# Layer 1 of a two-layer graph kernel reassociated, (A h) W in place of A (h W), with 512-wide matmuls

## What is computed

```python
h = jnp.maximum(_layernorm(x, axis=-1), 0.0)
Xw = h @ Wv + bv
sj = Xw @ aw[:d, 0]
si = Xw @ aw[d:, 0]
e = jax.nn.leaky_relu(sj[:, None, :] + si[:, :, None] + ab[0], negative_slope=0.2)
alpha_matrix = A * jnp.exp(e)
transition = alpha_matrix / (jnp.sum(alpha_matrix, axis=-1, keepdims=True) + 1e-12)
# H = sum over k of (transition^k h) @ Wk[k] + bk[k], for k = 0, 1, 2
x = x + jax.nn.relu(H)
h = jnp.maximum(_layernorm(x, axis=-1), 0.0)
Ah = A + jnp.eye(N)
dh = jax.lax.rsqrt(jnp.sum(Ah, axis=-1))
An = dh[:, :, None] * Ah * dh[:, None, :]
x = x + jax.nn.relu(jnp.einsum('bnm,bmf,fc->bnc', An, h, kernel) + bias)
```

## Time and profile before

| | us |
|---|---|
| median of 3 runs | 867.5 (867.31 to 870.92) |
| the profiled execution's own time | 868.26 |
| its span, first to last instruction | 866.5 |
| PE busy | 795.5 (92%) |
| DVE busy | 649.6 (75%) |
| ACT busy | 509.9 (59%) |
| POOL busy | 367.3 (42%) |
| DMA moved | 128.70 MB, mean 149 GB/s |

### The profile page before, as it was taken

How to read it: one execution, slowest core, us unless ns; L and a number is a source line. 1 busy time by engine, 2 the same in 40 slices (tenths; PEclk the granted TensorE clock), 3 DMA queues, 4 the chain that set the end, 5 groups by cost and what they waited for, 6 DMA issues and landing times.

```text
span 866.5 us, 15910 instructions
## 1 busy us (share of the span) xinstructions
PE 795.5 (92%) x6092; PEld 762.3 (88%) x6092; DVE 649.6 (75%) x1375; ACT 509.9 (59%) x997; POOL 367.3 (42%) x279
## 2 busy tenths in 40 slices
PE   2957999899989999899998999989998999999998
PEld 2757898898989999898998989889898999989998
DVE  4558597966979669885879759797697966986565
ACT  2488555676467654674647745567646765468232
POOL 1025154462355432652437515446235543275416
PEclk9968999999999999999999999999999999999999
DMA  5436341871428533574317834187143751256502
GB/s 182 146 120 196 134 129 44 254 246 61 135 84 252 201 98 98 153 257 157 114 52 223 272 102 128 44 255 244 62 134 88 250 210 37 99 164 205 187 30 98
DMA packets 65227, 128.70 MB, mean 149 GB/s; under 512 B 6272, under 2 KB 32256, under 8 KB 65152
## 3 DMA queue, kind: packets, MB, share of 16 engines
q1 hardware_dynamic: 55936, 94.13, 33.1%
q10 hardware_dynamic: 9216, 33.56, 13.0%
HBM read 119.28 MB, written 8.39 MB: 147 GB/s over the span
## 4 chain that ended last, share of the span: by engine, by line
PE 55%; DVE 27%; DMA 6%; issue 5%; ACT 5%; POOL 2%; ACTq 0%; DVEq 0%
PE da L818 12%; PE acc L907 12%; PE acc L909 11%; PE acc L908 11%; DVE tg_e L615 5%; PE db L818 5%; DVE a_raw L658 4%; DVE p L644 4%; DVE h L567 3%; DMA x_res<-x_dram 3%; DMA out_dram<-o_tile 2%; PE tp L810 2%; DVE p L639 2%; DVE ht_lo L586 2%; ACT t_hi L401 2%
## 5 line engine op out<-in xcount | busy, mean ns | idle before, releaser
L907 PE MATMUL acc<-g_hi,t_hi 128*128 128x256 f32 (+1 forms) x1024 | 294.6, 288 | 17.4 <-issue 10.6
L909 PE MATMUL acc<-g_hi,t_lo 128*128 128x256 f32 (+1 forms) x1024 | 291.4, 285 | 0.0
L908 PE MATMUL acc<-g_lo,t_hi 128*128 128x256 f32 x1024 | 290.2, 283 | 0.0
L309 POOL TENSOR_TENSOR a_lo<-a_raw,a_hi 128x512 fp32r<-128x512 f32 x128 | 186.3, 1473 | 176.9 <-ACT a_hi L442 175.4
L907 PEld LDWEIGHTS acc<-g_hi,t_hi 128*128 128x128 f32 x1024 | 195.6, 191 | 17.7 <-issue 10.7
L908 PEld LDWEIGHTS acc<-g_lo,t_hi 128*128 128x128 f32 x1024 | 195.8, 191 | 0.0
L909 PEld LDWEIGHTS acc<-g_hi,t_lo 128*128 128x128 f32 x1024 | 195.7, 191 | 0.0
L907 PE MATMUL acc<-g_hi,a_hi 128*128 128x256 f32 x512 | 149.2, 291 | 21.7 <-POOL a_lo L309 21.6
L909 PE MATMUL acc<-g_hi,a_lo 128*128 128x256 f32 x512 | 146.2, 285 | 0.0
L908 PE MATMUL acc<-g_lo,a_hi 128*128 128x256 f32 x512 | 146.1, 285 | 0.0
L391 ACT ACTIVATE tg_e<-si,sij 128x256 f32<-128x256 f32 x256 | 110.0, 500 | 56.4 <-POOL t_lo L315 52.7
(11 more groups left out here) (87 smaller groups left out, 1545.4 us busy)
## 6 DMA issues: line engine op xcount, KB each, us to landing
tg_a<-adj_t_dram ACTq DMA_DIRECT2D x64, 512.0 KB, 4.0
a_raw<-adj_dram SPq DMA_DIRECT2D x64, 512.0 KB, 4.6
a_raw<-adj_t_dram SPq DMA_DIRECT2D x64, 512.0 KB, 5.1
h<-x_dram SPq DMA_DIRECT2D x8, 1024.0 KB, 5.4
x_res<-x_dram SPq DMA_DIRECT2D x64, 128.0 KB, 3.7
out_dram<-o_tile SPq DMA_DIRECT2D x64, 128.0 KB, 3.4
p<-wk_dram SPq DMA_DIRECT2D x1, 768.0 KB, 7.2
p<-bk_dram SPq DMA_DIRECT2D x1, 384.0 KB, 7.5
```

Source lines behind the costliest of these rows:

```text
L309: nc.gpsimd.tensor_tensor(a_half(a_lo, i, h), a_raw[:, i % RS, h * N // 2:(h + 1) * N // 2], a_half(a_hi, i, h).bitcast(F32), ALU.subtract ...
L907: nc.tensor.matmul(acc[:, s, 0:n], l_hi, r_hi, start=(jt == 0), stop=False)
L908: nc.tensor.matmul(acc[:, s, 0:D], l_hi, r_lo, start=False, stop=False)
L909: ins = nc.tensor.matmul(acc[:, s, 0:n], l_lo, r_hi, start=False, stop=(jt == NT - 1))
```

## The change

Layer 1 is computed as (A h) W. After V, ACT makes h and its scaled high part from x (`h1_part`: two dependent activations), DVE the low part (`hs_low`). The transposes and `layer1_dense` before Z are gone. In Z the stationary operand is a 128x128 block of scaled h, the moving operand 512 columns of transposed adjacency: 16 pieces q of six matmuls (`layer1_piece`), pieces 0 to 7 for the first 512 rows into both banks of `da`, 8 to 15 for the others into both of `tp`. The result is z transposed; `zt_round` and `zt_low` split it, and W is multiplied last, in eight `out_chunk`s of six matmuls of 256 columns into the single bank `db`: chunks 0 to 3 after pieces 10 to 13, chunks 4 to 7 after chunks 1 to 4 of the next batch's U. T is stored in units of half the rows: the leaky relu is two instructions of 512 columns in place of four of 256, chunk 0 of U waits for four units and chunk 4 for all eight. The queues of SP, ACT, DVE and POOL are laid out anew. h of layer 0 (`h0`) and scaled h of layer 1 share one buffer, and `tmp` takes the place of `g1_tmp` and `h1`. The host lays the transposed adjacency out as `adj_z`, whose chunk is one run of 4 KB per partition, of the same bytes in all.

```diff
...
     T_D = {2: HALVES[0:1], 3: HALVES[1:2]}
-    T_V = {-1: HALVES[2:3], 1: HALVES[3:4], 2: HALVES[4:5], 3: HALVES[5:6], 4: HALVES[6:7]}
-    T_Z = {i: HALVES[7 + i:8 + i] for i in range(8)}
-    T_U = {i: HALVES[15 + i:16 + i] for i in range(3)}
-    BEFORE_U = 15
...
-    ROWS_U = {0: (0,), 1: (1,), 2: (2,), 3: (3, 4), 4: (5, 6), 5: (7,)}
...
-    DIAG_Z = {0: 4, 1: 5, 3: 6, 4: 7}
...
-    A_FIRST = {i: (i + 2, 1) for i in (0, 2, 3, 4, 5)} | {1: (4, 0)}
-    A_THEN = {0: (3, 1)} | {i: (i + 3, 0) for i in (2, 3, 4)}
+    T_V = {1: HALVES[2:3], 4: HALVES[3:4], 5: HALVES[4:5], 6: HALVES[5:6], 7: HALVES[6:7]}
+    T_Z = dict(zip((1, 3, 5, 6, 8, 10, 11, 13, 15), (HALVES[7 + i:8 + i] for i in range(9))))
+    T_U = {0: HALVES[16:17], 1: HALVES[17:18]}
+    BEFORE_U = 16
...
+    ROWS_U = {2: (0, 1), 3: (2,), 4: (3, 4), 5: (5, 6), 6: (7,)}
+    STATS_U = {2: (0, 1, 2, 3), 3: (4, 5, 6, 7)}
...
+    OUT_Z = {10 + i: i for i in range(PB)}
+    OUT_U = {1 + i: PB + i for i in range(PB)}
...
+    DIAG = (0, 1, NT - 2, NT - 1)
...
+        zt = [da, tp.rearrange("p g k i -> p g (k i)")]
+        zt_hi = ht_hi.rearrange("p g k i -> p g (k i)")
+        zt_lo = ht_lo.rearrange("p g k i -> p g (k i)")
...
+            def load_row(b, t):
+                if t >= RS:
+                    sp.wait_ge(rows_done, b * NT + t - RS + 1)
+                elif b > 0:
+                    sp.wait_ge(a_ready[1], (b - 1) * NT + NT - RS + t + 1)
+                sp.dma_start(a_raw[:, t % RS, :], adj_v[b, :, t]).then_inc(raw_loaded[t % RS], 16)
...
+                    sp.wait_ge(a_ready[1], b * NT + i - RS + 1)
+                sp.dma_start(a_raw[:, i % RS, :], adj_z[b, i]).then_inc(raw_loaded[i % RS], 16)
...
+                if b > 1:
+                    sp.wait_ge(a_used[1], (b - 1) * NT)
...
+            for b in range(B):
+                for i in range(RS):
+                    if b > 0:
+                        store(b - 1, PB + i)
+                    load_row(b, RS + i)
                 for i in range(RS):
                     load_chunk(b, i)
-                if left > 1:
+                for i in range(NT):
+                    load_x_res(b, i)
+                    if i in (RS, RS + 1):
+                        load_chunk(b, i)
+                load_chunk(b, RS + 2)
+                load_chunk(b, RS + 3)
+                for i in range(PB):
+                    if b + 1 < B:
+                        load_row(b + 1, i)
+                    store(b, i)
+                if b + 2 < B:
                     load_h0(b + 2)
...
+                act.wait_ge(raw_loaded[i % RS], 16 * (b * (2 * NT // RS) + NT // RS + i // RS + 1))
+                if i in DIAG:
+                    act.wait_ge(diag_done, b * len(DIAG) + DIAG.index(i) + 1)
+                if b * NT + i >= 2:
+                    act.wait_ge(a_used[h], b * NT + i - 1)
+                nc.scalar.copy(piece(a_hi, i % 2, h), piece(a_raw, i % RS, h)).then_inc(a_hi_done[h], 1)
+            def h1_part(b, m):
+                if m % 2 == 0:
+                    act.wait_ge(nb1_ready, b * NG + m // 2 + 1)
...
+                    act.wait_ge(hs_ready, b * NT + m - 1)
+                nc.scalar.activation(tmp[:, m % 2, :], p0[:, b % 2, m, :], ACT.Relu, bias=nb1[:, m:m + 1],
+                                     scale=rstd1[:, m:m + 1]).then_inc(h1_ready, 1)
+                if m == 0:
+                    act.wait_ge(dh_ready, b + 1)
+                act.wait_ge(h1_ready, b * NT + m + 1)
+                nc.scalar.activation(hs_hi[:, m, :], tmp[:, m % 2, :], ACT.Copy,
+                                     scale=dh[:, m:m + 1]).then_inc(hs_hi_done, 1)
+            def zt_round(b, r):
+                act.wait_ge(a_used[1], b * NT + (r + 1) * PB)
+                for d in range(KD):
+                    nc.scalar.copy(zt_hi[:, d, :], zt[r][:, d, :]).then_inc(zt_hi_done, 1)
...
+                for i in range(NT):
+                    if i == 0 and b > 0:
+                        zt_round(b - 1, 1)
+                    t_steps(b, T_U.get(i, ()))
+                    if i == NT - 1 and more:
+                        transposed_hi(b + 1, 0)
+                    act.wait_ge(g1_tmp_ready, b * NT + i + 1)
+                    nc.scalar.copy(g1_hi[:, i, :], tmp[:, i % 2, :]).then_inc(g1_hi_done, 1)
+                    for t in ROWS_U.get(i, ()):
+                        rows(b, t)
...
+                for i in range(NT):
+                    if i == 0:
+                        if more:
+                            si_copy(b + 1, NG - 1)
+                        a_round(b, 1, 0)
+                        a_round(b, 1, 1)
+                    if more:
+                        t_steps(b + 1, T_V.get(i, ()))
+                    if i >= 3:
+                        h1_part(b, i - 3)
+                for q in range(NP):
+                    if q < 3:
+                        h1_part(b, NT - 3 + q)
+                    if q == NP // 2:
+                        zt_round(b, 0)
+                    if q + 3 in range(4, NP):
+                        a_round(b, (q + 3) // 2, (q + 3) % 2)
+                    if more:
+                        t_steps(b + 1, T_Z.get(q, ()))
+            zt_round(B - 1, 1)
...
+            def hs_low(b, m):
+                dve.wait_ge(hs_hi_done, b * NT + m + 1)
+                nc.vector.scalar_tensor_tensor(out=hs_lo[:, m, :], in0=tmp[:, m % 2, :], scalar=dh[:, m:m + 1],
+                                               in1=hs_hi[:, m, :].bitcast(F32), op0=ALU.mult,
+                                               op1=ALU.subtract).then_inc(hs_ready, 1)
...
+            def zt_low(b, r):
+                for d in range(KD):
+                    dve.wait_ge(zt_hi_done, (2 * b + r) * KD + d + 1)
+                    nc.vector.tensor_tensor(zt_lo[:, d, :], zt[r][:, d, :], zt_hi[:, d, :].bitcast(F32),
+                                            ALU.subtract).then_inc(zt_ready, 1)
+            def out_chunk(b, i):
                 s = i % 2
-                dve.wait_ge(acc_full, b * PHASES + 2 * NT + i + 1)
-                nc.vector.scalar_tensor_tensor(out=z_tmp[:, s, :], in0=acc[:, acc_slot(Z_PHASE, i), 0:D], scalar=dh[:, i:i + 1],
+                dve.wait_ge(out_full, b * NT + i + 1)
+                if b * NT + i >= 2:
+                    dve.wait_ge(stored[s], 16 * (b * (NT // 2) + i // 2))
+                nc.vector.scalar_tensor_tensor(out=o_tile[:, s, :], in0=db[:, 0:D], scalar=dh[:, i:i + 1],
                                                in1=bias1[:, :], op0=ALU.mult, op1=ALU.add).then_inc(z_tmp_done, 1)
...
+                for i in range(NT):
+                    if i == 0 and b > 0:
+                        zt_low(b - 1, 1)
+                    if i == NT - 1 and more:
+                        transposed_lo(b + 1, 0)
+                    u_chunk(b, i)
+                    if b > 0 and i - 1 in OUT_U:
+                        out_chunk(b - 1, OUT_U[i - 1])
...
+                        if i == NORM_U:
+                            dve.wait_ge(rstd0_ready, b + 2)
+                            norm0(0)
+                            norm0(1)
...
+                for i in range(NT):
+                    v_chunk(b, i)
+                    if i % 2:
+                        moments(b * NG + i // 2 + 1, st1, mv1, ve1, stats1, mean1, ve1_ready, (i - 1, i))
+                    elif i > 0:
+                        bias_of_norm1(b, i // 2 - 1)
+                    if i >= 3:
+                        hs_low(b, i - 3)
+                    if more:
+                        t_steps(b + 1, T_V.get(i, ()))
+                bias_of_norm1(b, NG - 1)
+                for q in range(NP):
+                    if q < 3:
+                        hs_low(b, NT - 3 + q)
+                    if q in (3, 4):
+                        diag(b, q + 3)
+                    if q == NP // 2:
+                        zt_low(b, 0)
+                    if q - 1 in OUT_Z:
+                        out_chunk(b, OUT_Z[q - 1])
+                    if more:
+                        t_steps(b + 1, T_Z.get(q, ()))
+            zt_low(B - 1, 1)
+            for i in range(PB):
+                out_chunk(B - 1, PB + i)
...
             def layer0_dense(b):
+                if b > 0:
+                    pe.wait_ge(g1_tmp_ready, b * NT)
...
+            def out_chunk(b, i):
+                pe.wait_ge(zt_ready, (2 * b + i // PB + 1) * KD)
+                if i > 0:
+                    pe.wait_ge(z_tmp_done, b * NT + i)
+                c = slice(i % PB * P, (i % PB + 1) * P)
+                split_product(db, D, [(zt_hi[:, d, c], zt_lo[:, d, c], wl_hi[:, d, :], wl_lo[:, d, :])
+                                      for d in range(KD)]).then_inc(out_full, 1)
+            def layer1_piece(b, q):
+                r, jt, c, h = q // NT, q % NT, q // 2, q % 2
+                pe.wait_ge(a_ready[h], b * NT + c + 1)
+                if r == 0:
+                    pe.wait_ge(hs_ready, b * NT + jt + 1)
```

(20 more changed lines are left out.)

707 lines of the change are left out of this document (237 added, 470 removed).

## The result

The changed kernel takes **959.0 us** (median of 4 runs, 957.1 to 964.4) against 868.0 (867.3 to 870.9) for the kernel before, measured alternately on the same chip: a ratio of 1.1055, 95% interval 1.101 to 1.110. It is slower, by 91 us. The forecast was 969, the range 870 to 1010.

A forecast was written before the change was run, and what follows sets the result against it. PE was taken to set the pace in 66 of 103 us a batch, and a chain over ACT, DVE and POOL in Z. The terms summed to +101.5 us on the profiled 868.3, giving 969 us, range 870 to 1010.

The forecast's parts named there:

- Beginning: Start of the kernel: wider leaky relu steps shorten ACT's chain for T that PE waits for; -3 us (0 to -5).
- W in U: Four W chunks become extra PE work in each of seven U stages, 2.9 us each time; +20 us.
- Waits for `db`: In U, PE waits three times a batch until DVE has read the single bank; 4.5 us a batch, +31.5.
- the walk of Z: Z followed through the engines' queues, every tie given to POOL; it ended at 42.7 us, and 39 was taken.
- From U to D0: D0's head waits for `u_chunk(7)`, whose row load stands behind a store; 4 us a batch, +25 in all.
- Z: Layer 1 stage, taken as 39 us against 37.1: +2 a batch (-5 to +6), +14 in all.
- Clock: Lower granted clock behind the new waits, two losses of 0.8 us a batch: +1.6 a batch, +11 in all.
- End: Last batch: layer 1 shorter, -5 us; then a tail of z's split and four W chunks, 9.6 us, +8.
- the minimum of 32.1 us: Z's lower bound: piece 9, behind chunk 6's load, at 19.3 us without lag, then 12.8 of PE work.
- first rival: Only the shortest chains hold: DVE keeps pace in V, Z takes 32.1 us, no clock loss; 890 us, chance 0.25.
- second rival: PE's work decides, chunk 6's load doesn't hold piece 9, Z about 26 us; 848 us, chance 0.17.
- The port: DVE and POOL hinder each other; DVE's lag at V's end grows, and `hs_low` with two SBUF inputs worsens it.

The follow-up runs named there:

- e1: The changed kernel with the W chunks alternating between the two banks of `da` in place of the single bank `db`: 912.0 us.
- e2: The changed kernel with SP issuing each row tile's load before the store of the W chunk, in place of after it: 943.6 us.
- e3: The changed kernel with the identity added to chunks 6 and 7 at q = 7 and 8 in place of 3 and 4: 960.3 us.
- e14: e10 with Z's W chunks one piece later and three half steps of T moved from Z to U: 879.1 us.
- e11: The changed kernel with POOL subtracting only 128 of each 512 columns of the adjacency's low part, the other terms left out: 946.3 us.
- e8: The changed kernel with two banks, row loads first, last bias first, a later `g1_tmp` wait, and pieces prepared at q + 4 in place of q + 3: 880.4 us.
- e10: e8 with the identity added to chunks 6 and 7 at q = 6 and 7 in place of 3 and 4: 885.4 us.
- e15: e14 with the identity of chunks 6 and 7 added back at q = 3 and 4: 892.0 us.

## Why the prediction was right, step by step

The sign and the size were right, and the profile shows every wait that was named: in U before `out_chunk` three times a batch, at D0's head, before pieces 4, 5 and 9. That the sum came within 10 us is in part luck: two of its terms are wrong by over 20 us each, in opposite directions. Measured between the two profiled executions, whose spans differ by 89.7:

- **Beginning**, forecast -3: 0. D0 of batch 1 starts at 88.72 before and at 88.78 after. PE waits 17.0 us for `t_lo` ahead of its first chunk of U, since that chunk now needs four whole units. T's last low part is ready at 75.0, before it was 81.3, so the shorter leaky relu did its work. I had not priced the new condition on chunk 0, which lets PE start its first chunk only at 58.6, in place of 53.1, and which stands in the change.
- **W in U**, +20: as forecast. A chunk takes 0.71 to 0.72.
- **Waits for `db`**, +31.5: 7 x 3 x 1.45 = 30.5 in U. e1 confirms the cause. Ten more of them, 10.3 us, lie in Z (seven) and at the end (three); there the walk of Z and the tail had them.
- **From U to D0**, +25: 18.1, seven waits of up to 3.2. The kind is right (e2). From batch 1 on the wait is 2.6 to 3.2 us where I took 4; the rows land after 4.1 us where I took 4.6, and the rest of the difference isn't traced.
- **Z**, forecast +2 a batch, from a walk to 42.7: +0.5, and 3.4 us of the 37.6 are the clock. Without clock losses Z is 34.2, so the walk was 8 us too long and the value taken, 39, 5 too long. The bias of the last norm came at V's end + 6.2, not 7.9 (DVE starts it at 368.21), piece 5 at 12.7 (14.1), piece 9 at 21.9 (24.4). I had let every tie go against Z.
- **Clock**, +1.6 a batch: 1.5 in D0 and 3.4 in Z of batch 2, three times as much. Over the seven batches it is 29 us in Z and 7.5 in D0, against 11. I had misread. The stretch 256 to 262 with its 0.87 doesn't lie behind the stall of 2.1 us; the stall is in it and ends at 260.35. Cut there, the kernel before shows the lower clock behind this stall too, for 3.2 us, a loss of 1.6 and not of 0.8:

```profile
260.35:262.00 1.65, 1.65 (x8) 1.65 (x9) 1.65 (x3) 0.46 (x2) 1.27 (x1) 0.51 1.07 383
262.00:263.30 1.30, 1.30 (x8) 1.30 (x8) 1.30 (x2) 1.30 (x4) 0.80 (x1) 0.50 0.91 212
```

So this term is some 26 us too small and the one under Z some 35 too large (7 x 5), and most of the two cancels.
- **End**, -5 + 8 = +3: from V's end to the end of the span 956.2 - 915.6 = 40.6 against 866.5 - 831.7 = 34.8, +5.8. Layer 1 of the last batch is 27.0 against 31.5, as forecast; from the last matmul of Z to DVE's last instruction it is 11.5 in place of the 9.6 that I had, again by the clock:

```profile
949.18 0.55 PE L699 MATMUL db<-wl_hi,ht_hi 128*128 128x256 f32 x1 [0.67 <-DVE o_tile L591]
951.47 0.55 PE L699 MATMUL db<-wl_hi,ht_hi 128*128 128x256 f32 x1 [0.67 <-DVE o_tile L591]
```

The last W chunks start 2.29 apart, of which only 0.67 is wait; their matmuls start 0.21 apart where it is 0.12 at full clock.

By stages the difference of 89.7 us is: beginning and batch 0 -0.1; U of batches 1 to 7 with the waits behind it 241.3 against 7 x 23.8, +75; six D0, 119.7 against 6 x 19.1, +5; V +0.3; six Z, 225.2 against 6 x 37.1, +3; end +6. Of U's 75, 20 is work, 30.5 the bank and 17 the wait for D0, by the list of waits. Of the other 7 us, 5 are the 0.24 by which each of the 21 waits for the bank costs more than the list says (see e1), and 1 is the same at D0's head (0.17 each). One is left.

**The steps that failed** are the reading of the clock, above, and the one under Z that said that chunk 6's load, `diag`, product and rounding make the minimum of 32.1 us. The chain is there, link by link, and it does set piece 9. But it isn't what alone sets the length of Z: taken away (e3), Z stays. The first rival (890 us) priced Z at 32.1, a length that only e14 comes near (32.7), in which three T steps are gone from Z, the waits for `db` are gone and the lead is longer. The second rival let the whole kernel decide at this one point ("where piece 9 comes before 13 us"). Piece 9 comes at 21.9, so its condition wasn't met. In e3, where piece 9 doesn't wait, it still comes 20.9 us behind V's end, as piece 5 waits longer, and the kernel is as slow: to free chunk 6's chain is not enough.

**The port**: "lag grows rather than shrinks" was wrong as a forecast. The lock itself is there after too: a step of DVE with two SBUF inputs took 2.09 us beside POOL's instruction of 2.39, like the earlier trace rows, and 0.43 alone. This agrees with the Trainium skill (SBUF — State Buffer, section Who interferes with whom), which says that a VectorE instruction with two SBUF inputs contends with a GpSimd instruction that reads SBUF, and that whichever of the two issues first decides who blocks. (POOL's had begun first, at 353.67, DVE's at 354.26.) But the new layout has fewer collisions. DVE's product took 1.67 us on average before and takes 1.30, the addition of the identity 1.04 and now 0.36, and `hs_low`, the new instruction with two SBUF inputs that I had held against the edit, takes 0.51 against the 0.48 of `l1_low` (its shortest is 0.48). Three groups of DVE in the changed kernel, with shapes, count, busy time and mean ns:

```profile
L522 DVE TENSOR_TENSOR tg_e<-tg_a,tg_e 128x1024 f32<-128x1024 f32 x64 | 82.9, 1296 | 6.3 <-ACT tg_e L354 6.2
...
L566 DVE SCALAR_TENSOR_TENSOR hs_lo<-tmp,dh,hs_hi 128x256 fp32r<-128x256 f32 x64 | 32.9, 514 | 26.4 <-ACT hs_hi L398 26.4
L577 DVE TENSOR_TENSOR a_raw<-a_raw,ident 128x128 f32<-128x128 f32 x64 | 20.2, 356 | 46.8 <-DMA a_raw<-adj_z_dram 46.8
```

The last row's 46.8 us of DMA wait is what e3 took away, at no gain.

**What is shown and what is argued.** Shown: the bank (e1, 47 us), the row load (e2, 15.5 us), that with the early identity POOL's split isn't what holds Z (e11), and that the late identity pays only with fewer steps of T in Z (e3, e8, e10, e14, e15). Argued: that the reason is two chains of nearly the same length; the port of DVE and POOL stands as a rival (e3), and a run of e3 or e10 with the narrow split of e11 would be the test. Argued too: what is left in Z of e14, 30.5 us of waits for `a_lo` in `da` (pieces 4 to 6, behind the late norm of the last rows). No run moves that norm ahead of V's end. Left open: why DVE waits longer for that store in batch 6 of e14.

## What to carry to other kernels

Matmuls moved into a stage that PE fills alone cost their work and, with one bank, a handover to the engine that reads them each time: give them two banks before anything else, and look in every queue for what was put ahead of an older duty, here a store ahead of a load. When a stage is held by a chain, list the second-longest chain too before you price the removal of the first, and ask what the engines that it frees will collide with: here the removal of the first gave nothing alone, and paid only with T's steps thinned out. Price a stall of TensorE from start to start and by the slower matmuls behind it. And when you read a clock behind a stall, cut the window at the end of the stall.

## What was not expected of the hardware

- The clock behind a stall is worth some half of the stall. Waits of 2.6 to 3.6 us were followed by granted clocks of 0.50 to 0.69 over the next 3 to 5 us; in D0 that cost 1.5 us for a stall of 2.6 to 3.2 (20.2 against 18.7), in Z 3.4 us for 8.6 us of waits. The length of the last stall alone doesn't tell: behind 1.4 us (e2, D0), 2.4 us (e14, Z) and one of 2.77 us (D0 of the changed kernel) the clock is 1.00, and behind 2.1 us (the kernel before, 260.35) and behind 1.10 and 1.65 us close together (e14, 699.54) it is 0.50.
- Taking 114 us of work off POOL (e11) gave 13 us, and the engine that the list of waits names as PE's releaser was itself waiting for ACT (246 us of idle time before these instructions).
- DVE's small additions of the identity took 1.04 us on average before and 0.36 after, with no change to the instruction; its shortest is 0.28 in both. Those of 1.37 us in the kernel before stand beside POOL's splits of the adjacency, so some two thirds of their time goes to the port by this estimate. When e3 moved them, they rose to 0.69.
